# Second attention of a two-layer block: sums and spread one step later, and a product of the identity ahead of each shift and each group of sums

## The reference

```
x = x + ln(attention0(ln(x)))   # 16 heads of 128, weights of 4-bit codes and scales, no mask
x = x + ln(ffn0(ln(x)))         # gated, 704 hidden
x = x + ln(attention1(ln(x)))   # 16 heads of 16, causal
x = x + ln(moe(ln(x)))          # 16 experts, top 8, 2 shared
```

```
qkv = x @ w_attn + b_attn
att = softmax(where(causal, q k^T / sqrt(16), -inf))
return (att v) @ w_proj + b_proj
```

## Time and profile before

| | us |
|---|---|
| median of 3 runs | 1918.38 |
| lowest and highest | 1917.7, 1922.43 |
| the profiled execution, its own time | 1922.7 |
| its span in the trace | 1921.0 |
| the second attention in it | some 1235 to 1600 |

### The profile page before, as it was taken

How to read it: one execution, slowest core, us unless ns; L and a number is a source line. 1 busy time by engine, 2 the same in 40 slices (tenths; PEclk the granted TensorE clock), 3 DMA queues, 4 the chain that set the end, 5 groups by cost and what they waited for, 6 DMA issues and landing times. The chain is left out here.

```text
span 1921.0 us, 31389 instructions
## 1 busy us (share of the span) xinstructions
PE 1859.7 (97%) x10631; PEld 1469.4 (76%) x10631; DVE 1427.5 (74%) x2322; ACT 1177.6 (61%) x1913; POOL 1170.4 (61%) x951
## 2 busy tenths in 40 slices
PE   8999999999999999999999899999999989999997
PEld 7788888888888888888888778745555547888886
DVE  7787888888888888888878855577777767755556
ACT  5676666676666666766666766376666765533333
POOL 3786786777777767867766875234344436554445
PEclk9999999999999999999999999999998999999999
DMA  6787778778778777777777620000000011110001
GB/s 207 265 282 260 259 274 281 255 270 283 254 256 281 260 275 275 256 270 257 267 269 273 214 72 1 10 4 4 4 4 5 2 50 34 40 37 25 17 1 44
DMA packets 192675, 307.14 MB, mean 160 GB/s; under 512 B 11840, under 2 KB 151488, under 8 KB 192576
## 3 DMA queue, kind: packets, MB, share of 16 engines
q1 hardware_dynamic: 192576, 305.85, 45.8%
HBM read 170.54 MB, written 135.27 MB: 159 GB/s over the span
## 5 line engine op out<-in xcount | busy, mean ns | idle before, releaser
L656 POOL TENSOR_TENSOR attn_probT_lo<-attn_probT_lo,attn_probT_hi 128x1024 fp32r<-128x1024 f32 x251 | 604.5, 2409 | 186.8 <-ACT attn_probT_hi L1090 186.5
L1209 DVE STREAM_TRANSPOSE mlp_parts_home<-attn_prob 128x1024 f32<-128x1024 f32 x254 | 315.7, 1243 | 117.2 <-ACT attn_prob L1064 65.5
L1064 ACT ACTIVATE attn_prob<-psum,attn_neg_max 128x1024 f32<-128x1024 f32 x256 | 285.8, 1116 | 141.6 <-DVE attn_neg_max L1203 137.9
L1203 DVE TENSOR_REDUCE attn_neg_max<-psum 128x1 f32<-128x1024 f32 x256 | 305.7, 1194 | 21.4 <-PE psum L81 21.1
L1090 ACT ACTIVATE attn_probT_hi<-attn_probT_lo 128x1024 fp32r<-128x1024 f32 x251 | 263.8, 1052 | 0.5 <-DMA attn_probT_lo<-attn_spill 0.5
L81 PE MATMUL psum<-attn_probT_hi,attn_v_hi 128*128 128x512 f32 x512 | 204.5, 399 | 9.2 <-POOL attn_probT_lo L656 7.5
L81 PE MATMUL psum<-attn_probT_lo,attn_v_hi 128*128 128x512 f32 x512 | 203.7, 398 | 0.0
L81 PE MATMUL psum<-attn_probT_hi,attn_v_lo 128*128 128x512 f32 x512 | 202.9, 396 | 0.0
L81 PE MATMUL psum<-attn_key_hi,attn_q_hi 128*128 128x512 f32 x512 | 200.2, 391 | 2.4 <-ACT attn_prob L1064 2.2
L81 PE MATMUL psum<-attn_key_lo,attn_q_hi 128*128 128x512 f32 x512 | 201.3, 393 | 0.0
L81 PE MATMUL psum<-attn_key_hi,attn_q_lo 128*128 128x512 f32 x512 | 201.1, 393 | 0.0
(11 more groups left out here) (278 smaller groups left out, 4758.3 us busy)
## 6 DMA issues: line engine op xcount, KB each, us to landing
attn_spill<-mlp_parts_home SPq DMA_DIRECT2D x254, 512.0 KB, 4.7
attn_probT_lo<-attn_spill SPq DMA_DIRECT2D x254, 512.0 KB, 5.1
x_sb<-in_w_qkvo SPq DMA_DIRECT2D x30, 512.0 KB, 5.1
attn_v_all<-in_moe_w SPq DMA_DIRECT2D x24, 384.0 KB, 3.1
acc_sb<-in_x SPq DMA_DIRECT2D x4, 512.0 KB, 6.4
x_sb<-in_x SPq DMA_DIRECT2D x4, 512.0 KB, 6.3
out<-x_sb SPq DMA_DIRECT2D x3, 512.0 KB, 2.9
attn_bias_all<-in_b_qkv SPq DMA_DIRECT2D x8, 130.0 KB, 4.6
```

The costliest lines, as they stand in the source:

```text
L656: engine.tensor_tensor(lo, f32(lo), f32(hi), ALU.subtract).then_inc(done, 1)
L1064: nc.scalar.activation(to, by_key, ACT.Exp, bias=neg_max[:, tile % 2:tile % 2 + 1], accum_out=total[:, tile % half_tiles:tile % half_tiles ...
L1203: nc.vector.tensor_reduce(neg_max[:, tile % 2:tile % 2 + 1], scores(tile), AX.XY, ALU.max, negate=True).then_inc(max_ready, 1)
L1209: nc.vector.transpose(turned_prob[:, tile % 2, :], prob[:, tile % 2, :]).then_inc(turned, 1)
```

## The change

Four things are done. Sums, spread, y and output products of chunk 1 move one step later. Ahead of each of the stage's own shifts (15) and groups of sums (16), in the PSUM bank that they will overwrite, TensorE multiplies the identity with itself four times over, 512 columns in one product of 128x128 weights (`keep_pace`). ScalarE takes one exponential of a single column at the stage's start. And the memset of v goes from VectorE to GpSimd. The shift of half 0, chunk 0, lies in the stage before and gets no product.

```diff
     small_work = {
         0: [("stack", 1, 1, 0), ("stack", 1, 1, 1)],
-        1: [("shift", 0, 1, 0), ("sums", -1, 1, 0), ("stack", 1, 1, 2), ("stack", 1, 1, 3)],
-        2: [("spread", -1, 1, 0)],
-        3: [("project", 2, 0, 0)],
-        4: [("shift", 1, 0, 0), ("out", -1, 1, 0)],
-        5: [("out", -1, 1, 1), ("sums", 0, 0, 0)],
-        6: [("spread", 0, 0, 0)],
+        1: [("shift", 0, 1, 0), ("stack", 1, 1, 2), ("stack", 1, 1, 3)],
+        2: [("sums", -1, 1, 0)],
+        3: [("project", 2, 0, 0), ("spread", -1, 1, 0)],
+        4: [("shift", 1, 0, 0)],
+        5: [("out", -1, 1, 0), ("sums", 0, 0, 0)],
+        6: [("out", -1, 1, 1), ("spread", 0, 0, 0)],
...
-    Y_AT = {3: (1, 1), 7: (0, 0)}
+    Y_AT = {4: (1, 1), 7: (0, 0)}
...
+    PACED = ("sums", "shift",)
...
             moe.final.prepare(pool)
+            for i in range(2):
+                nc.gpsimd.memset(v[i][:, :, :, (1 - i) * D1:(2 - i) * D1], 1.0)
...
+            def keep_pace(bank):
+                nc.tensor.matmul(bank, ident_r[:], ident_r[:].unsqueeze(1).broadcast_to([P, NB // P, P]), start=True, stop=True)
...
                     wait_turn(pe, ("small", use))
                     at = of * chunks + c
+                    if kind in PACED:
+                        keep_pace(misc)
...
+            nc.scalar.activation(probT[:, 0, 0:1], k.ident[:, 0:1], ACT.Exp)
             for g in range(-FIRST, TOTAL + len(moe.steps) + 2):
...
-            for i in range(2):
-                nc.vector.memset(v[i][:, :, :, (1 - i) * D1:(2 - i) * D1], 1.0)
```

## The result

The changed kernel is slower than the kernel before by 0.3%: the median of 18 runs is 1927.24 us against 1921.82 us of 18 runs of the kernel before in turn with them, a ratio of 1.0029 [1.0018, 1.0039]. I had forecast 1914.9 us, a little faster, with a range up to 1923.5. The sign was wrong and the time is outside the range. Part of that distance is the starting point: I had applied the sum to a median of 3 runs, 1918.38 us, and the 18 runs have 3.4 us more. One run each of two later experiments (e6, 2966 us, and e12, 2036 us) was disturbed and is left out of every figure.

What follows compares the result with a forecast made beforehand. TensorE was taken as the bound, though not by much. Start -1.2, clock -1.5 and -6.0, products +5.6 and later sums -0.4 gave -3.5 us, from 1918.38 to 1914.9 us; eight-in-ten range 1908 to 1923.5.

Steps and rivals of the forecast that it cites:

- the later sums, "-0.4": Moving sums, spread, y and output products a step later was to give -0.4 us, bounds -2.9 and +4.2.
- The clock's term, "-6.0": Four low-clock units behind step 1 of halves 3, 4 and 5 were to go, 1.5 us each, -6.0 us.
- The five units that I let go: 3.4 us stretches at 1.2 GHz: four behind step 1 of halves 3 to 5, one at 1252; 1.5 us each.
- The products, "+5.6": The 31 identity products take 7.4 us of TensorE; three quarters were to count, +5.6 us.
- The start, "-1.2" and "-1.5": At the stage's start, the table load off the chain gives -1.2 us, the low-clock unit at 1252 gone -1.5 us.
- The clock falls as before: Rival, chance 0.18: new low-clock stretches come for those that go; +4.0 us, 1922.4 us.
- the ScalarE rival: Rival, chance 0.11: the spread's copy delays exponentials in steps 3 and 4 of 7 halves, +12.6; +9.5 us, 1927.9 us.
- The hidden products: Rival, chance 0.26: TensorE's waits for VectorE take in most of the products' time; -8.8 us, 1909.6 us.
- the 1.13 us of the earlier trace: TensorE's wait at step 1 of half 5 in the kernel before; most of it was to stay.
- my three signs of a wrong forecast: Stage clock still 0.96, exponential waits at step 4 or 5 over 4 us, or VectorE waits down by the products' time.

Runs made afterwards that it cites:

- e6: The kernel before with the early exponential, the memset on GpSimd and 16 identity products, ahead of the sums alone; ratio 0.9972.
- e12: The kernel before with the early exponential, the memset on GpSimd, and y and its output products one step later; sums and spread stay; ratio 1.0006.
- e2: The kernel before with the new order alone: later sums, spread, y and output products; ratio 1.0030.
- e1: The kernel before with the 31 identity products alone; ratio 0.9997.
- e3: The kernel before with the early one-column exponential and the memset on GpSimd alone; ratio 0.9981.
- e7: The changed kernel with norm work of half 2 and half 6 moved one step later; ratio 0.9994 to the kernel before.
- e8: The kernel before with four identity products in each place, 124 in all, and nothing else changed; ratio 1.0117 from 4 runs.

## Why the prediction was wrong, point by point

The forecast was the sum -3.5 us, and the kernel gave +5.6. Sorted by path and clock, I had +4.0 of path (-1.2 + 5.6 - 0.4) and -7.5 of clock (-1.5 - 6.0). Measured are +7.0 and -1.4, or +5.8 and +0.1 with the other base. So 2 to 3 us of the miss are path and 6 to 7.5 clock: the larger part is clock.

**The step that failed first: the later sums, "-0.4".** The order alone has +5.4 us, +3.7 of path and +1.7 of clock (e2). The sentence that failed is "y on GpSimd starts a step later, and its readers move with it". The readers did move, but the other work on the same queue did not: the norm's scaling stood behind y and now stands ahead of it, with its own wait of 2.28 us for VectorE. What it cost is less plain than that: TensorE's waits of half 6 sum to 5.8 us as before, and the half loses its 2.9 us by 3.5 us more at the low clock and four products. In the same way I weighed the spread's copy against the slack in half 4, where there is no piece of the norm, and not in half 2, where four instructions that take 2.08 us together stand beside it and the waits grow by 1.1 us. I had written both ends of a range (-2.9 to +4.2), and the path's +3.7 lies in it near the upper end. The rows of half 4 were the wrong rows: they show the slack of a half in which no piece of the norm is queued. Nowhere had I set the norm's pieces against the moved ones, half by half.

**The clock's term, "-6.0".** The units behind step 1 of halves 3, 4 and 5 did go, as I had said, and that of 1252 too. My reason for them is not shown: parting sums and shift does it (e2), products without parting do it (e1), and the start alone takes away two of the four units (e3). For the size of the term two things were wrong. One is the price: 3.4 us at 1.2 GHz lower the mean clock of a span of 1921 us by 3.4 / 2 / 1921 = 0.0009, and at 1.16 us per 0.001 they cost 1.0 us, near the 1.06 us of half 4. I took 1.5, from a stretch of wide products in which TensorE is the bound at every moment. The five units that I let go were worth some 5 us and not 7.5. The other is that I counted what would go and nothing that would come: each of the two new stalls is followed by low clock, 3.4 us at 1360 and 6.9 at 1542, where 3.4 stood at 1549. Moving the norm's pieces gives 2.8 us of clock back in the means (e7), though the trace of e7 has 20 us at the low clock against 24, with 6.8 of them at 1560 and new ones at 1382 and 1484. Why the changed kernel's mean clock is only 0.9926 stays open in the main: 1330 has 6.9 us at the low clock where it had 3.4, behind the same wait of 1.27 us, and 1600 is new, with no stall that I can tie to the order.

**The products, "+5.6".** Right in sum: 5.4 by e1 and 0.20 each by e8, which is 6.2. The chain of half 2 shows one: product and shift take 0.84 us where the shift alone took 0.59, 0.25 more and not 0.43.

**The start, "-1.2" and "-1.5".** Right in kind and 1.1 us short: 1.9 of path and 1.9 of clock (e3). The bounds (-1.3 and -1.5) left out that the memset might bring something, for which I had -1.0 as a bound. How the 1.9 us of path divide between table load and memset was not tried.

**The rivals.** "The clock falls as before" with 0.18 was the nearest in the difference (+4.0 against +5.4 by the medians) and in what happened: new low stretches came for those that went, 24 us against 27. Its cause (sparse work that falls elsewhere in time) was not tried. That 1927.24 us is close to the ScalarE rival's 1927.9 is luck, since 3.4 us of it are the starting point. ScalarE as the bound was right as a mechanism, with the wait at step 4 that I had named, but in one half of seven, 1.2 us and not 12.6. The hidden products fell: TensorE's waits for VectorE went from 11.1 to 8.9 us, 2.2 against 7.4 added, and that is the order's doing, 9.2 in e2 and 10.6 in e1. None of the three was GpSimd's queue, which by e12 may make the larger part of the order's cost.

**What I said would show it.** The clock is 1.00 behind step 1 of halves 3 to 5 and at the first exponentials: right. The stage's mean was to be 0.98 and is 0.97. The products start 0.34 us ahead of the shift, not 0.25, and last 0.50 us in the timeline, not 0.4. There is a wait of over 0.5 us at half 5, step 1. Here I had said two things, that most of the 1.13 us would stay and that no wait of over 0.5 us would be left, and the first was right:

```profile
1485.34 0.50 PE L2246 MATMUL psum<-attn_qk_hi,attn_to_stack 64*128 64x512 f32 x2 [1.47 <-issue]
```

It is the 1.13 us of the earlier trace rows, a little longer, and the clock stays at 1.00 there (the window of 1480 to 1490 above), where the kernel before had 6.8 us at the low clock. And none of my three signs of a wrong forecast came: the stage's mean is 0.97 and not 0.96, the waits for the exponentials at the output and v products sum to 2.3 us and not 4, and those for VectorE fall by 2.2 us and not by 7.4. All three asked after the rivals that I had thought of, and none after GpSimd.

On the clock both traces now speak against a single cause. In the kernel before, TensorE was busy nearly all of the time ahead of 1396 and of 1440, at the full clock (first and second row here), and the clock fell right behind, to a mean of 0.57 and 0.72:

```profile
1390.00:1396.00 6.00, 5.97 (x55) 3.61 (x54) 4.28 (x10) 2.20 (x5) 2.19 (x6) 1.00 0.01 3
1434.00:1440.00 6.00, 5.74 (x53) 3.45 (x53) 4.83 (x11) 3.31 (x8) 2.26 (x6) 1.00 0.00 0
```

In the changed kernel it fell at 1362 and 1542, behind 2.10 and 1.88 us of idle time, and did not fall behind 1.47 us at 1485. The Trainium skill, page "TensorE: Matmul & The Clock Gate", section "Why this matters for your kernels", sets the loss in mid-kernel down to idle gaps between bursts of matmuls, and the gaps that it names are longer than any in this stage. So the falls at 1362 and 1542 agree with its kind of cause and not with its size, as do those that the prediction counted for it at 1252, 1330 and 1480, and the falls at 1396 and 1440 do not agree at all.

## What to carry to other kernels

Before a piece of work is moved by one step, list for every engine queue what else stands in the new step, in each repetition and not in one: here one piece of the norm on ScalarE and one on GpSimd, each in one half, met the moved work in the two halves that lose 3 us each, and moving them in turn made VectorE's piece a new stall. Add up all waits of a stretch before a new one is called a cost: the 1.88 us for y stood in place of 1.65 us of older waits. Sort a comparison into path and clock by runs of one kernel at different clocks, and keep the uncertainty of each part beside it. And a wide product put in to hold the clock pays only where it costs less path (0.2 us each) than the clock that it holds: 31 of them about broke even, 16 may have given 1 us, and moving the sums behind the stack, with none, measured the same.

## What the runs showed of the hardware that I had not expected

- The spread of one kernel's time, 1913 to 1928 us, goes with its mean granted clock: 1925.7 us at 0.9885 and 1917.9 us at 0.9952. The same program spends more or less of its time at the low clock in different runs.
- The clock fell at 1396 with TensorE busy 5.97 of the 6 us ahead and no wait in them, behind 1.6 us of narrow products. Products of 512 columns ahead of each narrow group raise the mean clock from 0.9912 (35 runs without) to 0.9963 (12 runs with them), though TensorE's waits for VectorE only fall from 11.1 to 10.6 us.
- Three further products in each place (e8, 4 runs) show no higher clock: 0.9940.
- 3.4 us at 1.2 GHz cost half 4 of this kernel 1.06 us (42.03 against 40.97 us).
- A lone product of 512 columns takes 0.43 us on the chain and 0.17 to 0.21 us of the kernel's time, by the estimate of the path's part; two in a row start 0.24 us apart.
